# The first pair's filter step of a whitening and spectral filter kernel: six PSUM banks in turn, the soft threshold on ScalarE, the third pair whitened beside it

## The chip, the cores and the metric

The kernel runs on one core of one Trainium2 chip. The metric is device time in microseconds (us), the median of repeated runs. TensorE multiplies matrices into PSUM (8 banks), VectorE and ScalarE move PSUM to SBUF and do elementwise work, GpSimd does elementwise work in SBUF only, and SyncE issues the transfers. Everything is in 32-bit floats.

## The reference

The input x is (16, 56, 56, 64). First it is whitened over its 64 channels: the covariance over all tokens, a Cholesky factor, its inverse applied to each token, then gamma and beta. The second part is a block with a spectral filter:

```
h  = layer_norm(x, n1_g, n1_b)
xf = rfft2(h)                                  # over the two space axes
o1 = relu(block-diagonal complex layer(xf, w1, b1))
o2 = block-diagonal complex layer(o1, w2, b2)
y  = irfft2(softshrink(o2, 0.01))              # softshrink(v) = v - clamp(v, -lam, lam)
h  = y + h + x
out = gelu(layer_norm(h, n2_g, n2_b) @ mw1 + mb1) @ mw2 + mb2 + h
```

## The kernel before

**Tiling.** The 16 images go through in 8 pairs (PAIRS), one pair on 112 or 128 partitions. Before the first step there is a stage for all pairs: covariance, then elimination, which gives the whitening matrix wy. Then pairs 0 and 1 are whitened (SECOND_WHITEN is the list of banks of pair 1), and pair 0 is normalised.

**Steps.** After that the kernel runs `step(i)` for i = 0 to 7, then the last MLP. Each engine has its own `step` function, an order written out by hand; semaphores join them. Step i does the filter of pair i: `dft_h(i)` is already done, then `dft_w`, `layer_1`, `layer_2`, the soft threshold, `inv_w`, `inv_h`, and `dft_h(i + 1)`. Between these are spread the MLP of pair i-1 in seven slices, the transposes of pair i+2 (`transpose_x`, evicted by ScalarE's `ev_x`), the whitening of pair i+1 (`whiten`, `whiten_two`, evicted by VectorE's `ev_whiten`), and its first layer norm (`ln1_stats`, `mean_rstd`, `ln1_subtract`, `ln1_rstd`). Step 0 has no MLP beside it, and in it pair 1 is already whitened, so only the transposes of pair 2 and the norm of pair 1 stand beside the filter. Pair 2 is whitened in step 1.

**Layer 2 and soft threshold (L1137, L730, L736, L459).** Eight chunks, two at a time. TensorE writes two banks, VectorE adds the bias into `layer2` and clamps that into `clamped` (two buffers of each, L2_BUFS), and GpSimd subtracts the two into `p_y`. `y_ready` counts GpSimd's chunks; VectorE waits on it to reuse a buffer. `inv_w` (L1151) waits for all eight and is evicted by ScalarE (L1424). From layer 2 on, B_BANK gives every chunk bank 1 or 2 in turn: the other banks belong to the MLP and the whitening.

**Folded weights.** Once, in step 0 right after layer 1, TensorE computes two small products (L926, L929, in BANK_M, which is bank 3), and VectorE folds them into the MLP's bias and weights (L607, L608). ScalarE needs them before its first GELU in step 1.

**inv_h (L1183)** writes eight chunks, which VectorE adds to the residual (L758). In step 0 they lie in banks 1, 2, 4, 5, 6, 7, 1, 2 (`fin_bank`). `dft_h(1)` (L1089) reuses banks 4 to 7 as VectorE frees them, and needs all four passes of pair 1's norm (`norm1_step`). GpSimd's scaling of h (L438) waits for `dft_h` (`pe_h`); its residual (L433) stands between the scalings.

**Transfers.** SyncE loads a pair when the transposes of the pair before are done (`pe_a`).

## Time and profile before

| what | value |
|---|---|
| median of 3 runs | 781.53 us (779.47 to 782.99) |
| the profiled execution | 779.6 us |
| its span in the trace | 777.8 us |
| TensorE busy | 710.2 us, 91% |
| VectorE busy | 566.6 us, 73% |
| ScalarE busy | 388.7 us, 50% |
| GpSimd busy | 276.3 us, 36% |
| mean granted TensorE clock | 0.966 of 2.4 GHz |

The trace comes from one execution. A busy share is a mean over the whole span; the change touches the stretch from about 148 us to about 260 us, steps 0 and 1. A time below is counted from the span's start. PE is TensorE, DVE VectorE, ACT ScalarE and POOL GpSimd. L12 is line 12 of the kernel before. A granted clock of 1.00 is 2.4 GHz, of 0.50 is 1.2 GHz; a value between them is a stretch with both.

### The profile page before, as it was taken

How to read it: one execution, taken by the hardware profiler on the slowest of the kernel's cores; microseconds unless marked ns; L12 is line 12 of the kernel's file. 1: busy time of each engine (PE TensorE's matmuls, PEld its weight loads, DVE VectorE, ACT ScalarE, POOL GpSimd, SP SyncE). 2: the span in 40 equal slices, each digit the busy share in tenths (PEclk: the TensorE clock that was granted, in tenths of full speed). 3: DMA queues.
4: the chain of work that ended last, by engine and by line, in shares of the span. 5: the costliest groups of instructions: out<-in, count | busy, mean ns of one | idle time of the engine just before them, and what ended most of it. 6: DMA issues, size and time to landing. Idle time of an engine off the chain costs nothing.

```text
span 777.8 us, 29382 instructions
## 1 busy us (share of the span) xinstructions
PE 710.2 (91%) x12889; PEld 449.3 (58%) x12889; DVE 566.6 (73%) x1845; ACT 388.7 (50%) x709; POOL 276.3 (36%) x158
## 2 busy tenths in 40 slices
PE   6988999777789999999999999999999889899797
PEld 5986556746655665565555655555556555545343
DVE  4565998958789677967895879587958894951651
ACT  0012004642376657565765566566656545746265
POOL 7000000672564064406541563256235524560000
PEclk9898999897999999999999999999999999989989
DMA  9964000303000300030003000400100000001011
GB/s 247 269 154 144 3 3 5 82 3 84 3 3 25 109 27 15 27 109 27 15 27 109 27 14 26 114 32 5 37 27 27 9 32 25 27 15 37 13 44 63
DMA packets 11089, 40.07 MB, mean 52 GB/s; under 512 B 1955, under 2 KB 2083, under 8 KB 9507
## 3 DMA queue, kind: packets, MB, share of 16 engines
q1 hardware_dynamic: 10962, 38.20, 17.0%
q8 instruction: 102, 1.67, 0.9%
q14 instruction: 25, 0.20, 0.1%
HBM read 25.35 MB, written 12.85 MB: 49 GB/s over the span
## 4 chain that ended last, share of the span: by engine, by line
PE 64%; DVE 21%; ACT 8%; issue 5%; DMA 0%; POOL 0%; DVEq 0%; ACTq 0%
PE psum L1207 9%; PE psum L1216 9%; DVE stats L626 7%; PE psum L1183 6%; ACT o_g L1418 5%; PE psum L1151 5%; PE psum L1105 4%; PE psum L885 4%; PE psum L1089 3%; DVE layer L730 3%; PE psum L1196 3%; PE psum L936 3%; PE psum L1137 3%; PE psum L1225 3%; DVE oslice L745 2%
## 5 line engine op out<-in xcount | busy, mean ns | idle before, releaser
L1441 ACT ACTIVATE hid<-psum,hbias 128x448 f32<-128x448 f32 x224 | 124.8, 635 | 67.3 <-PE psum L1207 67.3
L1207 PE MATMUL psum<-n2T,mw1s 64*128 64x448 f32 x448 | 105.6, 583 | 6.9 <-ACT o_g L1418 6.2
L438 POOL TENSOR_TENSOR hbuf<-hbuf,prm 128x896 f32<-128x896 f32 (+1 forms) x29 | 53.5, 1848 | 159.4 <-PE psum L1089 159.4
L459 POOL TENSOR_TENSOR p_y<-layer,clamped 128x512 f32<-128x512 f32 (+1 forms) x64 | 75.9, 1185 | 74.4 <-DVE clamped L736 74.4
L1216 PE MATMUL psum<-hid,prm 128*64 128x448 f32 x448 | 96.3, 552 | 3.7 <-DVE oslice L745 3.6
L433 POOL TENSOR_TENSOR rbuf<-ybuf,prm 128x512 f32<-128x512 f32 (+2 forms) x10 | 32.4, 3236 | 157.5 <-DVE hbuf L857 128.2
L1151 PEld LDWEIGHTS psum<-cst,p_y 58*64 58x64 f32 x2048 | 52.6, 138 | 22.5 <-issue 21.2
L1151 PE MATMUL psum<-cst,p_y 58*64 58x112 f32 x2048 | 62.7, 269 | 2.8 <-ACT o_g L1424 2.5
L1450 ACT ACTIVATE mlp_t<-psum,prm 128x448 f32<-128x448 f32 x56 | 35.5, 635 | 58.4 <-PE psum L1216 56.9
L1207 PEld LDWEIGHTS psum<-n2T,mw1s 64*128 64x128 f32 x448 | 40.5, 192 | 36.2 <-issue 25.5
L1183 PE MATMUL psum<-o_g,cst 58*128 58x448 f32 x256 | 55.6, 554 | 2.0 <-ACT o_g L1424 1.2
L1122 PE MATMUL psum<-p_y,w1s 64*128 64x435 f32 (+1 forms) x256 | 53.0, 542 | 4.4 <-ACT o_g L1418 3.9
L626 DVE BATCH_NORM_STATS2 stats<-ybuf 128x6 f32<-128x64 f32 x392 | 51.7, 205 | 0.9 <-ACT ybuf L1541 0.9
L1216 PEld LDWEIGHTS psum<-hid,prm 128*64 128x64 f32 x448 | 27.2, 136 | 42.4 <-issue 31.0
L1433 ACT COPY n2T<-psum 128x448 f32<-128x448 f32 x56 | 29.9, 533 | 42.9 <-PE psum L1196 42.6
L1137 PE MATMUL psum<-w2s,o_g 64*64 64x64 f32 x1856 | 37.6, 223 | 14.6 <-DVE layer L730 12.8
L1137 PEld LDWEIGHTS psum<-w2s,o_g 64*64 64x64 f32 x1856 | 31.7, 134 | 32.4 <-DVE layer L730 20.6
L936 PE MATMUL psum<-cst 64*64 64x128 f32 x714 | 49.9, 306 | 0.5 <-issue 0.5
L1418 ACT ACTIVATE o_g<-psum,prm 64x435 f32<-64x435 f32 (+1 forms) x80 | 49.4, 618 | 1.3
L730 DVE TENSOR_TENSOR layer<-psum,prm 128x512 f32<-128x512 f32 (+1 forms) x64 | 40.4, 632 | 11.9 <-PE psum L1137 11.8
L758 DVE TENSOR_TENSOR fbuf<-psum,fbuf 128x448 f32<-128x448 f32 x32 | 18.5, 619 | 41.8 <-PE psum L1183 41.8
L1396 ACT COPY u_r<-psum 120x464 f32<-120x464 f32 x64 | 31.6, 550 | 34.4 <-PE psum L1089 34.2
(140 smaller groups left out, 1363.0 us busy)
## 6 DMA issues: line engine op xcount, KB each, us to landing
xin<-x_dram SPq DMA_DIRECT2D x8, 1568.0 KB, 8.7
out_dram<-oslice SPq DMA_DIRECT2D x112, 112.0 KB
ybuf<-x_dram SPq DMA_DIRECT2D x2, 1568.0 KB, 16.9
fbuf<-x_dram SPq DMA_DIRECT2D x2, 1568.0 KB, 20.1
xin<-x_dram SPq DMA_DIRECT2D x4, 392.0 KB, 5.4
n<-x_dram SPq DMA_DIRECT2D x1, 1568.0 KB, 23.4
n<-x_dram SPq DMA_DIRECT2D x4, 392.0 KB, 16.4
prm<-params_dram SPq DMA_DIRECT2D x1, 646.0 KB, 3.9
```

The source lines that it names most:

```text
L438: nc.gpsimd.tensor_tensor(h4[:, j0:j1], h4[:, j0:j1], gain[:, j0:j1].unsqueeze(2).broadcast_to((RP, j1 - j0, W, 2)), ALU.mult).then_inc(h_ ...
L459: nc.gpsimd.tensor_tensor(yk, a, b, ALU.subtract).then_inc(y_ready, 1)
L626: last = nc.vector.bn_stats(stats[:, w, :], src[:, w * C:(w + 1) * C])
L730: nc.vector.tensor_tensor(layer2[:, c % L2_BUFS, 0:n].rearrange("p (k m) -> p k m", m=C), bank[B_BANK[L2 + c]][:, 0:n].rearrange("p (k m) ...
L936: nc.tensor.matmul(t[cols, 128:128 + 128], ident[rows, 0:C], ident[rows, 0:128], start=True, stop=True, skip_group_check=True)
L1137: one = nc.tensor.matmul(t[b][C * half:C * half + C, j * C:j * C + C], o_g[C * b:C * b + C, at:at + C], w2s[C * b:C * b + C, C * half:C * ...
L1151: one = nc.tensor.matmul(t[h][C * d:C * d + C, j * 112:j * 112 + 112], y_v[rows, CH // 2 * s + 4 * k + j, C * d:C * d + C], cc("invw")[row ...
L1183: one = nc.tensor.matmul(t[d][:, 0:7 * C], cc("invh")[rows, RP * m:RP * m + RP], g[rows], start=(m == 0), stop=(m == 1))
L1207: nc.tensor.matmul(t[:, 0:4 * ROWS], mw1s[C * v:C * v + C, HH * m:HH * m + HH], n2T[C * v:C * v + C, s % 2, :], start=True, stop=True).the ...
L1216: last = nc.tensor.matmul(t[C * v:C * v + C, 0:4 * ROWS], pp("mw2")[:, C * m:C * m + C], hid[:, s % 2, m, v, :], start=(m == 0), stop=(m = ...
L1418: last = nc.scalar.activation(dst, src, ACT.Relu, bias=bias)
L1441: nc.scalar.activation(hid[:, s % 2, m, v, :], bank[CH_MLP[i].bank[k]][:, 0:4 * ROWS], ACT.Gelu, bias=hbias[:, m:m + 1]).then_inc(c_act, 1)
```

## The change

All of it is in step 0 and what follows from that.

- `step(0)` becomes `first_step` on TensorE, VectorE and ScalarE, with an order of its own.
- The transposes of pair 2 and their evictions move from layer 2 and `inv_w` to between the parts of `dft_w`; they use banks 0 and 3 in turn.
- In step 0, layer 2 and `inv_w` go through six banks in turn (`FIRST_SPECTRAL`) and not two.
- The soft threshold of step 0: VectorE only adds the bias; ScalarE computes relu(-v - lam) and relu(v - lam) (`shrink_first`), the second one in place; GpSimd subtracts them. There are three pairs of buffers and they lie in `hid`, the MLP's space, which is not in use yet.
- The whitening of pair 2 moves from step 1 into step 0, between the chunks of layer 2, through banks 0 and 3 (`THIRD_WHITEN`). Steps 2 and later are as before.
- `folded_weights` moves: on TensorE from behind layer 1 to behind `inv_w`, and it waits for pair 2's whitening; on VectorE to behind layer 2's evictions and ahead of `mean_rstd(1, 0)` and pair 1's norm.
- One constant, `minus_lam`, is set by GpSimd at the start.

```diff
-    return BANK_M if i == 1 and k % 2 == 1 else BANK_X
+    return BANK_M if 0 < i < 3 and k % 2 == 1 else BANK_X
...
+THIRD_WHITEN = (BANK_X, BANK_M, BANK_X, BANK_M, BANK_X, BANK_M, BANK_X)
 WHITEN = (BANK_X, 1, 2, BANK_X, 1, 2, BANK_X)
+FIRST_SPECTRAL = ((1, 2), (6, 7), (4, 5))
...
+def whiten_bank(i, k):
+
+    return (FIRST_WHITEN, SECOND_WHITEN, THIRD_WHITEN, WHITEN)[min(i, 3)][k]
+
+
+def spectral_bank(i, k):
+
+    return FIRST_SPECTRAL[(k - L2) // 2 % 3][k % 2] if i == 0 else B_BANK[k]
...
+        def shrink_bufs(i, c):
+
+            if i == 0:
+                spare = hid[:].rearrange("p s m v n -> p (s m v n)")
+                return [spare[:, 512 * j:512 * j + 512] for j in (c % 3 * 2, c % 3 * 2 + 1)]
+            return [layer2[:, c % L2_BUFS, :], clamped[:, c % L2_BUFS, :]]
...
-                        a, b = (m[:, c % L2_BUFS, 0:n].rearrange("p (k s j) -> p k s j", s=2, j=CH) for m in (layer2, clamped))
+                        a, b = (m[:, 0:n].rearrange("p (k s j) -> p k s j", s=2, j=CH) for m in shrink_bufs(i, c))
...
-                        dve.wait_ge(r_begun, 3 * i - 2)
+                        dve.wait_ge(r_begun, 3 * i - 2 if i > 2 else 1)
...
-                            bank[(WHITEN if i > 1 else SECOND_WHITEN)[k]].rearrange("p (w c) -> p w c", c=C),
+                            bank[whiten_bank(i, k)].rearrange("p (w c) -> p w c", c=C),
...
-                        if c >= L2_BUFS or i > 0:
-
-                            dve.wait_ge(y_ready, i * 8 + c - L2_BUFS + 1)
+                        bufs = 3 if i == 0 else L2_BUFS
+                        if c >= bufs or i > 0:
+
+                            dve.wait_ge(y_ready, i * 8 + c - bufs + 1)
                         n = L2_KH[c // 2] * C
+                        value, bound = shrink_bufs(i, c)
                         nc.vector.tensor_tensor(
-                            layer2[:, c % L2_BUFS, 0:n].rearrange("p (k m) -> p k m", m=C),
-                            bank[B_BANK[L2 + c]][:, 0:n].rearrange("p (k m) -> p k m", m=C),
+                            value[:, 0:n].rearrange("p (k m) -> p k m", m=C),
+                            bank[spectral_bank(i, L2 + c)][:, 0:n].rearrange("p (k m) -> p k m", m=C),
...
+                        if i == 0:
+                            continue
                         dve.wait_ge(b_dve, i * B_DVE + b_done("dve", L2 + c))
-                        nc.vector.tensor_scalar(clamped[:, c % L2_BUFS, 0:n], layer2[:, c % L2_BUFS, 0:n], LAM, -LAM,
+                        nc.vector.tensor_scalar(bound[:, 0:n], value[:, 0:n], LAM, -LAM,
...
+                def first_step():
+
+                    ev_layer_1(0)
+                    ev_whiten(2, [0])
+                    ev_layer_2(0, [0, 1])
+                    ev_whiten(2, [1, 2])
+                    ev_layer_2(0, [2, 3])
+                    ev_whiten(2, [3, 4])
+                    ev_layer_2(0, [4, 5])
+                    ev_whiten(2, [5, 6])
+                    ev_layer_2(0, [6, 7])
+                    folded_weights()
+                    mean_rstd(1, 0)
+                    for k in range(2):
+                        ln1_subtract(1, k)
+                        ln1_rstd(1, k)
+                    ev_inv_h(0, range(8))
+                    for k in range(4):
+                        ln2_stats(0, k)
+
                 def step(i, ahead, behind):
...
-                        if i > 0:
+                        if i > 1:
...
-                    if i == 0:
-                        folded_weights()
...
-                    if i == 0:
-                        ev_inv_h(0, range(8))
-                        for k in range(4):
-                            ln2_stats(0, k)
-                        return
...
-                    pe.wait_ge(whitened, 2 * 7)
+                    pe.wait_ge(whitened, 3 * 7)
...
                             pe.wait_ge(*((whitened, 1 + 3 * k) if k < 2 else (a_act, 7 + k - 1)))
+                        elif i == 2 and k > 0:
+                            if k > 1:
...
                     for k in (2 * q + 1, 2 * q + 2):
-                        if q == 0:
+                        if i == 2:
+                            pe.wait_ge(whitened, 2 * 7 + 2 * q + 1)
...
-                                last = nc.tensor.matmul(bank[WHITEN[2 * q + 1 + v]][C * b:C * b + C, j * C:j * C + C],
+                                last = nc.tensor.matmul(bank[whiten_bank(i, 2 * q + 1 + v)][C * b:C * b + C, j * C:j * C + C],
...
+                def free_spectral(i, k):
+
+                    if i > 0:
+                        return free_b(i, k)
+                    if L2 + 6 <= k < INVW:
+                        pe.wait_ge(b_dve, b_done("dve", k - 6))
+                    if k >= INVW + 6:
+                        pe.wait_ge(b_act, b_done("act", k - 6))
+                    return bank[spectral_bank(i, k)]
+
...
-                    if k == 0 and i < PAIRS - 1:
+                    if k == 0 and 1 < i < PAIRS - 1:
                         pe.wait_ge(whitened, (i + 1) * 7 + 6)
-                    t = [free_b(i, L2 + 2 * k + b) for b in range(2)]
+                    t = [free_spectral(i, L2 + 2 * k + b) for b in range(2)]
                     for j in js:
...
-                    t = [free_b(i, INVW + 2 * k + h) for h in range(2)]
+                    t = [free_spectral(i, INVW + 2 * k + h) for h in range(2)]
...
 
+                def first_step():
+
+                    transpose_x(2, [0, 1])
+                    dft_w(0, 0)
+                    transpose_x(2, [2, 3])
+                    dft_w(0, 1)
+                    transpose_x(2, [4, 5])
+                    dft_w(0, 2)
+                    transpose_x(2, [6])
+                    layer_1(0, [0])
+                    dft_w(0, 3)
+                    layer_1(0, [2, 4, 6])
+                    whiten(2, [0])
+                    pe.wait_ge(b_act, b_done("act", L2 - 1))
+                    pe.wait_ge(b_dve, b_done("dve", L2 - 1))
+                    layer_2(0, 0, range(L2_KH[0]))
+                    layer_2(0, 1, range(L2_KH[1]))
+                    whiten_two(2, 0)
+                    layer_2(0, 2, range(L2_KH[2]))
+                    whiten_two(2, 1)
+                    layer_2(0, 3, range(L2_KH[3]))
+                    whiten_two(2, 2)
+                    for k in range(4):
+                        inv_w(0, k, range(4))
+                    folded_weights()
+                    for k in range(4):
+                        inv_h(0, k)
+                    for q in range(4):
+                        dft_h(1, q)
+
...
-                        if ahead and i > 0:
+                        if ahead and i > 1:
...
-                    if ahead and i > 0:
+                    if ahead and i > 1:
...
-                    if i == 0:
-                        folded_weights()
...
-                    if i == 0:
-                        inv_w(i, 3, range(4))
-                        for k in range(4):
-                            inv_h(i, k)
-                        for q in range(4):
-                            dft_h(i + 1, q)
-                        return
...
                     fill(3)
+
+                def shrink_first(c):
+                    n = L2_KH[c // 2] * C
+                    over, under = (m[:, 0:n] for m in shrink_bufs(0, c))
+                    act.wait_ge(b_dve, b_done("dve", L2 + c))
+                    nc.scalar.activation(under, over, ACT.Relu, bias=minus_lam[:], scale=-1.0)
+                    nc.scalar.activation(over, over, ACT.Relu, bias=minus_lam[:]).then_inc(shrunk, 1)
+
+                def first_step():
+
+                    ev_x(2, [0, 1])
+                    ev_dft_w(0, [0, 1])
+                    ev_x(2, [2, 3])
+                    ev_dft_w(0, [2, 3])
+                    ev_x(2, [4, 5])
+                    ev_dft_w(0, [4, 5])
+                    ev_x(2, [6])
+                    ev_dft_w(0, [6, 7])
+                    ev_layer_1(0)
+                    for c in range(8):
+                        shrink_first(c)
+                    ev_inv_w(0, range(8))
+                    for q in range(4):
+                        ev_dft_h(1, q)
```

## Rows read from the trace of the kernel before

**Rows 1.** Busy time by stage: us, busy us (and instructions) per engine, granted clock, DMA share, GB/s.
```profile
166.60:181.00 14.40, 8.07 (x256) 6.45 (x256) 12.25 (x19) 3.37 (x7) 9.56 (x8) 0.93 0.01 2
...
181.00:195.70 14.70, 10.99 (x260) 9.71 (x261) 10.62 (x18) 4.91 (x10) 0.00 (x0) 0.73 0.41 111
...
235.10:310.70 75.60, 72.48 (x1440) 44.39 (x1438) 59.26 (x194) 46.63 (x85) 32.74 (x19) 1.00 0.15 45
```

**Rows 2.** ScalarE in order of time: start us, us, instruction, count.
```profile
125.36 0.59 ACT L1541 COPY ybuf<-psum 128x512 f32<-128x512 f32 x1 [55.21 <-PE psum L1046]
...
160.27 6.33 ACT L1418 ACTIVATE o_g<-psum,prm 64x435 f32<-64x435 f32 x10
```

**Rows 3.** TensorE in order of time; in brackets the idle time before, and who ended it.
```profile
131.82 1.13 PE L1029 MATMUL psum<-cst,xin 112*128 112x112 f32 x8 [0.44 <-ACT xT L1390]
...
149.38 0.68 PE L1105 MATMUL psum<-cst,u_r 56*64 56x58 f32 x31 [1.12 <-ACT u_r L1396]
...
155.67 3.05 PE L1122 MATMUL psum<-p_y,w1s 64*128 64x435 f32 x8
...
164.77 0.68 PE L929 MATMUL psum<-mw1s,pilot_w 64*128 64x256 f32 x2
...
179.77 1.01 PE L1029 MATMUL psum<-cst,xin 112*128 112x112 f32 x4 [0.72 <-ACT xT L1390]
...
181.03 3.26 PE L1151 MATMUL psum<-cst,p_y 58*64 58x112 f32 x64 [0.25 <-POOL p_y L459]
...
192.78 1.76 PE L1151 MATMUL psum<-cst,p_y 58*64 58x112 f32 x64 [1.15 <-ACT o_g L1424]
...
195.70 6.53 PE L1183 MATMUL psum<-o_g,cst 58*128 58x448 f32 x32 [1.15 <-ACT o_g L1424]
```

**Rows 4.** VectorE in order of time, first step and start of the second.
```profile
168.60 0.43 DVE L736 TENSOR_SCALAR clamped<-layer 128x512 f32<-128x512 f32 x1
...
169.66 1.01 DVE L736 TENSOR_SCALAR clamped<-layer 128x512 f32<-128x512 f32 x1
...
179.82 0.24 DVE L646 TENSOR_TENSOR small<-stats 128x56 f32<-128x56 f32 x1
...
180.16 0.93 DVE L649 TENSOR_TENSOR small<-stats 128x56 f32<-128x56 f32 x1
...
183.98 2.02 DVE L687 TENSOR_TENSOR hbuf<-n,small 128x1792 f32<-128x1792 f32 x1
...
190.04 2.03 DVE L693 TENSOR_TENSOR hbuf<-hbuf,small 128x1792 f32<-128x1792 f32 x1
...
197.55 1.16 DVE L758 TENSOR_TENSOR rbuf<-psum,rbuf 128x448 f32<-128x448 f32 x2 [5.48 <-PE psum L1183]
...
210.27 2.18 DVE L646 TENSOR_TENSOR small<-stats 128x56 f32<-128x56 f32 x1
...
235.07 0.68 DVE L730 TENSOR_TENSOR layer<-psum,prm 128x512 f32<-128x512 f32 x1
```

**Rows 5.** GpSimd in order of time, first step and start of the second.
```profile
172.39 1.28 POOL L459 TENSOR_TENSOR p_y<-layer,clamped 128x512 f32<-128x512 f32 x1 [0.36 <-DVE clamped L736]
...
216.87 1.27 POOL L433 TENSOR_TENSOR fbuf<-n,prm 128x512 f32<-128x512 f32 x1
```

**Rows 6.** TensorE in order of time, step 1 around its whitening and layer 2.
```profile
226.66 1.02 PE L1207 MATMUL psum<-n2T,mw1s 64*128 64x448 f32 x4
...
228.02 1.16 PE L1064 MATMUL psum<-wy,xT 64*64 64x64 f32 x64 [0.34 <-DVE ybuf L711]
...
231.80 1.77 PE L1207 MATMUL psum<-n2T,mw1s 64*128 64x448 f32 x8
...
233.51 1.16 PE L1137 MATMUL psum<-w2s,o_g 64*64 64x64 f32 x64
```

**Rows 7.** TensorE alone in stretches of 0.5 us: busy us (instructions), granted clock, DMA share, GB/s.
```profile
178.50:179.00 0.50, 0.50 (x4) 0.84 0.00 0
...
189.00:189.50 0.50, 0.00 (x0) 0.92 0.92 258
```

More of the change, by code:

```diff
@@ L220, in build @@
         negm = sb("negm", [128, 1])
+        minus_lam = sb("minus_lam", [128, 1])
         CW = 130
@@ L423, in _ @@
                 nc.gpsimd.memset(xT[:], 0.0).then_inc(s_ones, 1)
+                nc.gpsimd.memset(minus_lam[:], -LAM).then_inc(s_ones, 1)
                 r4 = [t.rearrange("p (w j h) -> p w j h", j=CH, h=2) for t in rf]
@@ L862, in _ @@
                 first_h()
-                step(0, True, False)
+                first_step()
                 for i in range(1, PAIRS - 1):
@@ L1021, in transpose_x @@
                             pe.wait_ge(*((whitened, 1 + 3 * k) if k < 2 else (a_act, 7 + k - 1)))
+                        elif i == 2 and k > 0:
+                            if k > 1:
+                                pe.wait_ge(a_act, 2 * 7 + k - 1)
                         elif k > 0:
@@ L1042, in whiten @@
                             pe.wait_ge(b_dve, (i - 2) * B_DVE + b_done("dve", FIN + 5))
-                        t = bank[(FIRST_WHITEN, SECOND_WHITEN, WHITEN)[min(i, 2)][k]]
+                        t = bank[whiten_bank(i, k)]
                         for j in range(4):
@@ L1052, in whiten_two @@
                     for k in (2 * q + 1, 2 * q + 2):
-                        if q == 0:
+                        if i == 2:
+                            pe.wait_ge(whitened, 2 * 7 + 2 * q + 1)
+                        elif q == 0:
                             who = B_READERS[L1 + 3 + k][0]
@@ L1376, in _ @@
                     dft_h(0, q)
-                step(0, True, True, False)
+                first_step()
                 for i in range(1, PAIRS - 2):
@@ L1397, in ev_dft_h, with ev_dft_w @@
                             "p (j k s) -> p k s j", j=8, s=2)).then_inc(b_act, 1)
-                def ev_dft_w(i):
-                    for k in range(8):
+                def ev_dft_w(i, ks=range(8)):
+                    for k in ks:
                         act.wait_ge(pe_b, b_count(i, S2 + k))
@@ L1424, in ev_inv_w @@
                         nc.scalar.copy(g_v[:, :, k % 2, :, 4 * (k // 2):4 * (k // 2) + 4],
-                                       bank[B_BANK[INVW + k]][:, 0:448].rearrange("p (j w m) -> p m w j", j=4, m=2)).then_inc(b_act, 1)
+                                       bank[spectral_bank(i, INVW + k)][:, 0:448].rearrange("p (j w m) -> p m w j", j=4, m=2)).then_inc(b_act, 1)
                 def ev_n2(i, s):
@@ L1522, in step @@
                     slice_(6, lambda j: rows_next({0: 2, 1: 3}.get(j)))
-                act.wait_ge(s_ones, MEMSETS + 2)
+                act.wait_ge(s_ones, MEMSETS + 3)
                 for k in range(7):
@@ L1550, in _ @@
                     ev_dft_h(0, q)
-                step(0, True, False)
+                first_step()
                 act.wait_ge(s_mlp, 2)
```

## The prediction

> **What bounds the kernel now.** I read the spans by stage first, then the order of time on each engine between 125 and 236 us. From step 1 on, a step takes 75.6 us, in which TensorE is busy for 72.5 [rows 1]: a delay that is still there when that rhythm starts goes straight into the end. The first filter step runs with no MLP beside it, and there TensorE is busy for only 8.1 of 14.4 us (layer 2) and 11.0 of 14.7 us (inverse transform over w) [rows 1]. So what bounds it is latency, not work, and I follow who waits for whom.
>
> ScalarE's ten layer 1 evictions start at 160.27 and end at 166.6 [rows 2]; call this T. Layer 2 waits for them. Before, layer 2 then alternates with VectorE over two banks, and the last y is there at 181.0, T+14.4: the next TensorE instruction, 181.03, waits on GpSimd's last y [rows 3]. The pace in between is GpSimd's: one y chunk takes 1.28 us and another 0.36 idle for the clamp [rows 5]. The clamp takes 0.43 us alone and 1.01 while GpSimd works [rows 4]. inv_w goes from 181.03 to 195.70, with a wait of 1.15 us for ScalarE before each later part [rows 3]. Meanwhile VectorE does the second pair's norm, from 179.82 to 192.07 [rows 4]. It is then free, and idle for 5.48 us before the first inv_h eviction at 197.55; call this S [rows 4].
>
> **Third pair's transposes among dft_w.** Seven groups of transposes and seven evictions move out of layer 2 and inv_w. Two groups cost TensorE 1.13 us at 2.4 GHz, one costs 1.01 at 1.2 GHz [rows 3]. The first two groups fall into the 1.12 us idle ahead of dft_w at 149.38 [rows 3]. The other five lie in dft_w. Before, the granted clock is at the lower level there: layer_1's first eight matmuls take 3.05 us, half a 64x448 pace [rows 3], against 1.77 for eight of a similar size in step 1 [rows 6]. If filling the idle keeps the clock high, five groups cost 2.8 us and layer_1's first part gives back 1.3, dft_w some 1.5: about 0. If the clock falls all the same, five groups cost 5 us, of which the waits there can take 2: +2.8. I take 0, and keep -0.3 and +2.8. ScalarE has idle time for its seven, 0.6 us each, before the chain at 160.27.
>
> **Layer 2.** TensorE starts at T; a pair of chunks takes 1.16 us [rows 6]. VectorE evicts a chunk in 0.68 [rows 4] and has two whitening evictions of about the same size between pairs. In order: chunks 0, 1 at T+1.3 to 2.6; whitening 1, 2 ready at T+3.5, evicted by T+4.8; chunks 2, 3 by T+6.1; whitening 3, 4 by T+7.4; chunks 4, 5 by T+8.7; whitening 5, 6 by T+10; chunks 6, 7 by T+10.9. ScalarE's two sides have no row; the nearest is a copy of 128x512 in 0.59 us [rows 2], the lower bound, and GpSimd's 1.28 for such a chunk [rows 5] is the upper one for each side. I take 0.6 each, 1.2 a chunk, being nearest to the same engine's row: the last ends at T+12.3. GpSimd, without the clamp's 0.36, adds 1.3 a chunk behind it and ends at T+13.8. So y is ready at 180.4 against 181.0: only 0.6 us gained, because GpSimd sets the pace either way. At the upper bound ScalarE would pace, at 2.5 us a chunk, and y would come 6 us later still.
>
> The Trainium skill (ScalarE: Activation LUTs, Rules for kernel authors) speaks against this edit: it has such relu and min/max work on VectorE. Its cost formula there is 280 ns plus 0.833 ns an element, so 0.71 us a side; the sum by it would be some 0.5 us longer. The trace cannot show the new shape; it shows 0.59 for a plain copy [rows 2].
>
> **inv_w over six banks.** The three waits for ScalarE of 1.15 us go [rows 3]. 64 matmuls take 1.76 us at 2.4 GHz and 3.26 at 1.2 [rows 3], so the whole is 7.0 to 13.0 us. Ahead of it TensorE has nothing from about T+8.5 to T+13.8. Before, with smaller gaps, the clock fell at 178.8 and came back at 189.0, 8 us after inv_w began [rows 7]. I take half speed for six to seven of the first microseconds: 10 us. inv_w ends at 190.4, and after the last eviction inv_h can begin at 191.5, which is 4.2 us earlier than 195.70.
>
> **The new wait.** On TensorE folded_weights now stands behind inv_w. On VectorE it stands ahead of mean_rstd(1) and the four norm passes, and waits for TensorE's two products. Queued behind it: the norm, then every inv_h eviction. VectorE is done with layer 2 at T+10.9 = 177.5, and now idles until the products at about 191.5 (L929's part takes 0.68 [rows 3]). Then come two small instructions, together 0.6 by the nearest row, 0.43 for a 128x512 clamp [rows 4]; mean_rstd, 4.16 before, of which 0.68 was one instruction stretched to 0.93 beside GpSimd, so 3.5; and the norm passes from 183.98 to 192.07, 8.1 [rows 4]. 191.5 + 0.6 + 3.5 + 8.1 = 203.7. S moves from 197.55 to 203.7, **+6.1 us**. Work that was hidden by inv_w has lost its cover. dft_h of the second pair waits too: its banks are freed by these evictions.
>
> **After S.** inv_h's fourth part needs the banks of the first two evictions, S+1.2, and TensorE has then been idle for some 8 us. At 1.2 GHz it takes 3.3 rather than 1.65 us (1.65 is a fourth of the 6.53 us row [rows 3]), so dft_h starts at about S+4.5, and its first quarter ends 0.7 to 0.8 us later after S than before. GpSimd's scaling and residual follow that, and the small VectorE instructions of mean_rstd wait for them: the first takes 2.18 us at 210.27 [rows 4], and they run freely only once GpSimd's last residual, from 216.87, is over [rows 5]. +0.8.
>
> **Step 1 without whitening.** Its seven VectorE evictions and 200 TensorE instructions go. On the path that is less than their sum: n2 and layer 1 still have to come from VectorE. Between mlp_in at 226.66 and layer_2 at 233.51 lie 6.85 us [rows 6]. Without the whitening: two halves of 1.02, four GELUs and a copy on ScalarE, 1.77 for the next mlp_in: about 5.5. -1.3, and VectorE, which reaches layer 2 late by 0.4 before (235.07 against 233.51 + 1.16), is on time: -0.2 more. I take -1.5; bounds are 0 and the 4.5 us of VectorE's seven evictions.
>
> **Sum.** 0 + 6.1 + 0.8 - 1.5 = +5.4 us (the -0.6 and the -4.2 are inside the 6.1). The profiled execution took 779.6 us, span 777.8; it becomes 785.0. The median of the runs stands 1.9 us above it, so I forecast **786.9 us**.
>
> **Rivals.** (a) TensorE's clock stays at 2.4 GHz through inv_w: 7 us instead of 10, then +2.4 us, 783.9. For: the packed whitening before it; against: 5 us idle just ahead of it, and the fall at 178.8 with less. 0.15. (b) The end on the other side: the stretched small instructions after 210.27 meet GpSimd no more, because VectorE arrives later than GpSimd's residuals. They last 8 us before and some 1.2 free (five at the 0.24 of the row at 179.82 [rows 4]); 6.7 off gives -1.3, 780.2. It decides if GpSimd is done with its residual by S+13. Against: GpSimd's start hangs on dft_h, which S moves as well. 0.13. The Trainium skill (SBUF — State Buffer, Who interferes with whom) has the pair of engines share ports by an exclusive lock; the 0.43 against 1.01 us of the clamp [rows 4] agrees. (c) The clock stays low through the transposes and all of inv_w: +2.8 and +3.0, 792.7. 0.12. (d) ScalarE's two sides go at the upper bound: +6, 793. 0.04. The forecast itself, between +2.5 and +9 us (784.0 to 790.5), 0.50; something else, 0.06.
>
> **Chances and range.** 0.5% is 3.9 us, about what a measurement of this kernel can tell from no change; so slower begins at 785.4. Of the forecast's 0.50 I put 0.42 above it; with (c), (d) and some of the rest, slower has 0.60. The remaining 0.08, (a) and half of (b) give 0.31 for the same; faster has 0.09. The likeliest case's own range is 784.0 to 790.5; the range to hold 8 in 10 goes from 780.0, the value of (b), to 793.0, that of (c) and (d); past it lie their far halves and what I have not named.
>
> **What would show it.** VectorE idle for 12 to 15 us ahead of the folded weights (L607), released by TensorE; the norm passes after inv_w and not beside it; the first inv_h eviction near 204; TensorE idle for 7 to 9 us within inv_h; the last y near 180.4, with GpSimd's chunks 1.3 apart; inv_w about 10 us without a wait for ScalarE; step 1's layer 2 some 5 us later than 233.5; later steps 75.6 us as before. The forecast is wrong if y comes before 178, if VectorE's norm is not held by the folded weights, or if n2 of the first pair is ready before 226.

## The result

The changed kernel took 787.28 us (median of 4 runs, 786.94 to 791.43), the kernel before 780.52 (4 runs: the three behind the table above and one more). The ratio worked out from all these runs is 1.0103, with a 95% interval from 1.0067 to 1.0139 (the two medians alone give 1.0087): slower by 1.0%, which is above the 0.5% that a measurement can tell. The forecast was 786.9. It lies closer than it deserves: the measured difference is 6.8 us, the forecast one 5.4, and before's median is 1.0 us lower with the fourth run. The profiled execution took 786.94 us, its span is 785.0 (+7.2).

The spans by stage of the changed kernel: layer 2; then inv_w up to the first inv_h eviction; then one later step.

```profile
165.60:181.88 16.28, 7.47 (x425) 6.85 (x425) 8.36 (x15) 9.60 (x16) 9.31 (x8) 0.95 0.02 4
181.88:203.81 21.93, 14.79 (x286) 12.02 (x286) 11.44 (x22) 3.87 (x8) 0.00 (x0) 0.81 0.01 1
241.50:317.10 75.60, 71.06 (x1376) 43.34 (x1372) 57.26 (x191) 45.04 (x83) 32.70 (x19) 1.00 0.15 45
```

A stretch of 75.6 us holds one later step as before [rows 1]; counted from layer 2 to layer 2, steps 2 to 5 take 75.46 to 75.47 us, 75.44 to 75.69 before. So the loss lies ahead of them. TensorE of the changed kernel in order of time:

```profile
155.93 1.73 PE L1165 MATMUL psum<-p_y,w1s 64*128 64x435 f32 x8
...
168.66 0.50 PE L1190 MATMUL psum<-w2s,o_g 64*64 64x64 f32 x18 [1.22 <-issue]
...
172.22 0.50 PE L1190 MATMUL psum<-w2s,o_g 64*64 64x64 f32 x18 [1.46 <-issue]
...
181.88 8.94 PE L1204 MATMUL psum<-cst,p_y 58*64 58x112 f32 x256 [4.74 <-POOL p_y L480]
...
191.22 0.68 PE L967 MATMUL psum<-mw1s,pilot_w 64*128 64x256 f32 x2
191.99 4.78 PE L1236 MATMUL psum<-o_g,cst 58*128 58x448 f32 x24
205.11 3.35 PE L1236 MATMUL psum<-o_g,cst 58*128 58x448 f32 x8 [8.34 <-DVE rbuf L783]
208.39 3.54 PE L1132 MATMUL psum<-cst,hbuf 56*56 56x58 f32 x155
...
233.63 3.36 PE L1260 MATMUL psum<-n2T,mw1s 64*128 64x448 f32 x8 [3.44 <-DVE o_g L741]
...
240.36 1.16 PE L1190 MATMUL psum<-w2s,o_g 64*64 64x64 f32 x64
```

256 matmuls run through without a pause. Of the three waits of 1.15 us that the prediction counts, two stood inside inv_w, ahead of its third and fourth part, and are gone. Ahead of the second part the wait was only 0.22 us. TensorE of the kernel before:

```profile
185.45 3.27 PE L1151 MATMUL psum<-cst,p_y 58*64 58x112 f32 x64 [0.22 <-ACT o_g L1424]
189.87 1.76 PE L1151 MATMUL psum<-cst,p_y 58*64 58x112 f32 x64 [1.15 <-ACT o_g L1424]
```

The third, at 195.70 [rows 3], stands ahead of inv_h, which needs the last eviction of inv_w whatever the banks are: e2, e6 and e9 below still wait 1.17, 1.17 and 1.16 us there, and in the changed kernel the folded weights' products fill it. But inv_h, which starts at 191.99 and not at 195.70, stops after 24 matmuls for 8.34 us, for evictions. VectorE of the changed kernel over the same time says why:

```profile
191.93 0.16 DVE L628 TENSOR_TENSOR hbias<-psum,prm 128x2 f32<-128x2 f32 x1 [12.61 <-PE psum L967]
192.34 0.24 DVE L667 TENSOR_TENSOR small<-stats 128x56 f32<-128x56 f32 x1
...
195.81 2.03 DVE L708 TENSOR_TENSOR hbuf<-n,small 128x1792 f32<-128x1792 f32 x1
...
203.81 3.28 DVE L783 TENSOR_TENSOR rbuf<-psum,rbuf 128x448 f32<-128x448 f32 x6
...
216.75 2.67 DVE L667 TENSOR_TENSOR small<-stats 128x56 f32<-128x56 f32 x1
...
229.52 4.01 DVE L741 TENSOR_SCALAR o_g<-psum,prm 64x435 f32<-64x435 f32 x6
```

VectorE idles for 12.61 us, until L967 (L929 before), the folded weights' product that stands behind inv_w, is done. Only then do the second pair's norm passes begin, which ran beside inv_w before [rows 4]. In the view of the waits it is one row among many:

```profile
DVE fbuf L783 <- PE psum L1236: 43.5, 14, 8.4
...
DVE hbias L628 <- PE psum L967: 12.6, 1, 12.6
```

The first, 43.5 us, is larger but it is 14 waits of the later steps, where TensorE is the bound; 12.6 in one wait, in a stretch where TensorE is not, is the loss.

Since the kernels differ only between the first and the second step, I read every trace by five events: T, layer 2's start; y, inv_w's start; S, the first inv_h eviction; n2, the start of VectorE's layer 1 evictions behind n2 (229.52 above); L2, step 1's layer 2. T itself moved between 163.0 and 168.4 from one trace to another, e6 with 163.0 having before's code up to there; so in a single trace the stretches from T on say more than the span. e5 is not in the table: the execution that was traced took 818.0 us at a mean granted clock of 0.832, a slow one, where its other nine took 771.7 to 777.5. All in us:

| kernel | T | T to y | y to S | S to n2 | n2 to L2 | L2 to end | T to end |
|---|---|---|---|---|---|---|---|
| before | 166.66 | 14.37 | 16.52 | 24.99 | 10.97 | 544.3 | 611.1 |
| after | 165.60 | 16.28 | 21.93 | 25.71 | 10.84 | 544.6 | 619.4 |
| e1 | 164.63 | 14.28 | 12.37 | 24.79 | 12.43 | 545.0 | 608.9 |
| e2 | 167.24 | 14.39 | 11.70 | 24.77 | 12.43 | 543.2 | 606.5 |
| e3 | 164.76 | 12.52 | 20.81 | 25.65 | 12.07 | 546.6 | 617.6 |
| e4 | 163.83 | 15.87 | 21.42 | 25.72 | 10.82 | 545.0 | 618.9 |
| e6 | 162.97 | 14.35 | 14.66 | 27.94 | 12.68 | 545.5 | 615.1 |
| e7 | 167.95 | 15.43 | 11.35 | 24.46 | 10.84 | 542.3 | 604.4 |
| e8 | 168.38 | 15.98 | 10.80 | 24.79 | 10.42 | 541.4 | 603.4 |
| e9 | 164.06 | 14.38 | 10.97 | 23.85 | 10.98 | 542.1 | 602.2 |
| e10 | 164.86 | 14.08 | 11.03 | 23.96 | 9.54 | 543.1 | 601.7 |
| e11 | 165.22 | 12.62 | 11.36 | 23.41 | 11.90 | 543.0 | 602.3 |

Behind L2 all these kernels do the same work in the same order, and still that column moves by 5.2 us. Part of it is a pause of TensorE in step 1's MLP, released by nothing that the trace shows: 1.69 us in the changed kernel, 1.72, 0.43, 2.24 and 1.48 in e1 to e4, 1.81 in e6, and none at this place in before and in e7 to e11. TensorE of the changed kernel:

```profile
277.34 0.97 PE L1269 MATMUL psum<-hid,prm 128*64 128x448 f32 x4 [1.69 <-issue]
```

So a few us between two kernels in the last two columns are no effect of an edit until their medians say so too.

### The profile page after: what moved, and what is told of

Same layout as the page of the kernel before. It is cut to its first block, busy times and chain, and to the rows that moved or that the text cites. A ratio compares the mean times of both kernels' runs of the same rounds, so it can differ in the third digit from the quotient of the medians.

```text
span 785.0 us, 29380 instructions
## 1 busy us (share of the span) xinstructions
PE 706.0 (90%) x12889; PEld 447.3 (57%) x12889; DVE 559.3 (71%) x1837; ACT 397.3 (51%) x725; POOL 277.8 (35%) x159
## 4 chain that ended last, share of the span: by engine, by line
PE 63%; DVE 22%; ACT 8%; issue 6%; DMA 0%; POOL 0%; DVEq 0%; ACTq 0%
PE psum L1260 9%; PE psum L1269 8%; DVE stats L647 7%; PE psum L1236 6%; ACT o_g L1492 5%; PE psum L1204 5%; PE psum L923 4%; PE psum L1148 3%; PE psum L1132 3%; PE psum L1190 3%; PE psum L1278 3%; PE psum L974 3%; PE psum L1249 3%; DVE layer L753 2%; DVE oslice L770 2%
## 5 line engine op out<-in xcount | busy, mean ns | idle before, releaser
L480 POOL TENSOR_TENSOR p_y<-layer,clamped 128x512 f32<-128x512 f32 (+1 forms) x56 | 66.3, 1184 | 64.8 <-DVE clamped L761 64.8
L1204 PEld LDWEIGHTS psum<-cst,p_y 58*64 58x64 f32 x2048 | 52.3, 138 | 23.4 <-issue 17.8
L1236 PE MATMUL psum<-o_g,cst 58*128 58x448 f32 x256 | 57.2, 568 | 9.3 <-DVE rbuf L783 8.3
L783 DVE TENSOR_TENSOR fbuf<-psum,fbuf 128x448 f32<-128x448 f32 x32 | 18.5, 620 | 43.5 <-PE psum L1236 43.5
L1190 PEld LDWEIGHTS psum<-w2s,o_g 64*64 64x64 f32 x1856 | 32.0, 134 | 29.0 <-DVE layer L753 14.6
L1479 ACT ACTIVATE p_y<-psum,prm 128x464 f32<-128x464 f32 (+1 forms) x64 | 36.5, 611 | 19.9 <-PE psum L1148 19.9
## 6 DMA issues: line engine op xcount, KB each, us to landing
n<-x_dram SPq DMA_DIRECT2D x4, 392.0 KB, 14.1
```

The source lines that it names most:

```text
L480: nc.gpsimd.tensor_tensor(yk, a, b, ALU.subtract).then_inc(y_ready, 1)
L1190: one = nc.tensor.matmul(t[b][C * half:C * half + C, j * C:j * C + C], o_g[C * b:C * b + C, at:at + C], w2s[C * b:C * b + C, C * half:C * ...
L1204: one = nc.tensor.matmul(t[h][C * d:C * d + C, j * 112:j * 112 + 112], y_v[rows, CH // 2 * s + 4 * k + j, C * d:C * d + C], cc("invw")[row ...
L1236: one = nc.tensor.matmul(t[d][:, 0:7 * C], cc("invh")[rows, RP * m:RP * m + RP], g[rows], start=(m == 0), stop=(m == 1))
```

## The experiments

Ratios are against the kernel before, run on the same chip (its median was 777.9 to 778.6 us), with 95% intervals. All of them compute the whole result; the filler products in e8 to e11 go to a bank that holds nothing anyone still reads.

### Folded weights behind the norm (e1), and early on TensorE (e2)

e1 changes one place in VectorE's order:

```diff
     def first_step():                      # VectorE
-        folded_weights()
         mean_rstd(1, 0)
         for k in range(2):
             ln1_subtract(1, k)
             ln1_rstd(1, k)
+        folded_weights()
         ev_inv_h(0, range(8))
```

> The changed kernel with one edit: on VectorE the folded weights stand behind the second pair's norm, not ahead of it. Theory (the norm is held behind the folded weights): VectorE does the norm from about 179.3 to 191, beside inv_w, so the first inv_h eviction comes at about 193.8 instead of 203.8, and the whole is 10 us shorter, 777 us: below the kernel before (780.5). Rival (the loss is in the pauses inside layer 2 and in the low clock at step 1's first MLP product; VectorE's hold is covered): 785 us or more.

Measured: 775.58 us, ratio 0.9959 (0.9935 to 0.9983). y to S falls from 21.93 to 12.37 us. VectorE of e1, the norm now 14.6 us earlier, beside inv_w:

```profile
181.20 2.03 DVE L708 TENSOR_TENSOR hbuf<-n,small 128x1792 f32<-128x1792 f32 x1
...
189.37 0.16 DVE L628 TENSOR_TENSOR hbias<-psum,prm 128x2 f32<-128x2 f32 x1
...
191.28 1.16 DVE L783 TENSOR_TENSOR rbuf<-psum,rbuf 128x448 f32<-128x448 f32 x2 [1.42 <-PE psum L1236]
```

L628 no longer waits, and the eviction at 191.28 waits for inv_h (L1236) itself. One line's place cost 1.4% of the kernel, more than the whole loss; with it mended the change is faster than before.

e2 leaves VectorE's order and moves TensorE's side:

```diff
     whiten_two(2, 2)                       # TensorE, first_step
+    folded_weights()
 ...
     inv_w(0, ...)
-    folded_weights()
```

> The changed kernel with one edit: on TensorE the two small products stand ahead of inv_w, not behind it; VectorE's order stays. Theory: VectorE's two instructions run at about 180 and the norm behind them ends at about 191.5; same gain as the first experiment, 777 us, since it is the wait that costs and not the place in one engine's queue. inv_w then starts no later, because TensorE idles there anyway. Rival: the products delay inv_w by 1 us and the gain stays under 3 us, 784 us.

Measured: 775.1 us, 0.9975 (0.9946 to 1.0003). y to S is 11.70, and y is not delayed (T to y 14.39). TensorE of e2 shows the products in its idle time ahead of inv_w:

```profile
178.75 0.68 PE L967 MATMUL psum<-mw1s,pilot_w 64*128 64x256 f32 x2
181.63 8.69 PE L1204 MATMUL psum<-cst,p_y 58*64 58x112 f32 x256 [2.20 <-POOL p_y L480]
```

The interval just reaches 1, so e2 isn't shown to be faster than before, but it is clear of the changed kernel's. The wait is a matter of the two queues' orders against each other: either one mends it.

### The third pair's whitening back in step 1 (e3), and that with e1 (e5)

```diff
     def whiten_bank(i, k):
-        return (FIRST_WHITEN, SECOND_WHITEN, THIRD_WHITEN, WHITEN)[min(i, 3)][k]
+        return (FIRST_WHITEN, SECOND_WHITEN, WHITEN, WHITEN)[min(i, 3)][k]
     # first_step, TensorE and VectorE: no whiten(2, ..), no ev_whiten(2, ..)
     def whitened_next(*ks):
-        if i > 1:
+        if i > 0:
```

> The changed kernel with the third pair's whitening put back into step 1; all else as changed, the folded weights' wait too. Theory: without the 200 small instructions the pauses of 1.2 and 1.5 us inside layer 2 go, GpSimd sets the pace, and the last y is there 13.2 us after layer 2's start, not 16.3: 3 us gained there. In step 1 the whitening costs 0 to 1.5 us, since it fills waits. Together 784.5 to 785.5 us. Rival (moving the whitening is what the change gains by): 788 us or more.

Measured: 786.28 us, 1.0103 (1.0054 to 1.0152). The interval holds both sides' ratios, so the times decide nothing. The trace of e3 does show the parts. T to y falls to 12.52, with one pause of TensorE instead of two:

```profile
167.73 1.96 PE L1182 MATMUL psum<-w2s,o_g 64*64 64x64 f32 x114 [1.00 <-issue]
...
177.28 7.82 PE L1196 MATMUL psum<-cst,p_y 58*64 58x112 f32 x256 [7.59 <-POOL p_y L480]
...
226.56 1.16 PE L1099 MATMUL psum<-wy,xT 64*64 64x64 f32 x64 [2.15 <-DVE o_g L741]
227.85 1.65 PE L1252 MATMUL psum<-n2T,mw1s 64*128 64x448 f32 x4
229.43 1.99 PE L1099 MATMUL psum<-wy,xT 64*64 64x64 f32 x64
```

GpSimd of e3 takes the eight chunks without a gap:

```profile
168.11 9.12 POOL L480 TENSOR_TENSOR p_y<-hid 128x512 f32<-128x512 f32 x8 [4.37 <-ACT hid L1547]
```

n2 to L2 grows from 10.84 to 12.07. That the whitening itself needs this time isn't shown: TensorE idles for 2.15 us ahead of it, and then a group of four takes 1.65 us and a whitening group 1.99, against 1.02 and 1.16 before [rows 6]. So whitening in layer 2 costs 3.8 us there against this trace of the changed kernel, and 1.6 to 1.9 against those of e1, e2 and e10, whose layer 2 is the same; it saves 1.2 in step 1. From T to the end e3 is 1.8 us shorter; 2.0 are lost again behind L2, of which 0.55 is its longer pause in step 1. The rest has no cause that the trace shows.

> The first and third experiments together: folded weights behind the norm on VectorE, and the third pair's whitening in step 1 as before. Kept of the change: six banks, threshold on ScalarE, transposes among dft_w. Theory (the parts add up by stretches): layer 2 to the last y 12.5 us, y to the first inv_h eviction 12.0, to n2 24.8, to step 1's layer 2 about 11.5; together 60.8 us, against 66.9 before and 63.9 in the first experiment: 6 us under the kernel before, a ratio near 0.992. Rival (moving the whitening is worth having once the hold is gone): slower than the first experiment, ratio 0.996 or more.

Measured (e5, both edits): 772.95 us, 0.9937 (0.9912 to 0.9961). The point is on my theory's side of 0.996 and the interval just reaches it; e1's interval overlaps. Only its times are used. Where the whitening stands is worth little either way.

### The clamp back on VectorE (e4)

```diff
     # ev_layer_2
-        if i == 0:
-            continue
     # ScalarE, first_step
-        for c in range(8):
-            shrink_first(c)
```

> The changed kernel with the soft threshold as before, one clamp on VectorE, in the new buffers; nothing on ScalarE. Theory (ScalarE's two sides gain little): VectorE takes 4.1 us for a pair of chunks with its whitening, the last y is there at 16.4 us after layer 2's start against 16.3, 787 us, within 1 us of the changed kernel. Rival (two-sided threshold on ScalarE is the gain of the change): y 3 us or more later, 790 us.

Measured: 785.48 us, 1.0099 (1.0060 to 1.0137), T to y 15.87 against 16.28. Putting the threshold on ScalarE gained and cost nothing that these times can tell. The two orders have different limits, though. ScalarE and GpSimd of the changed kernel, one view for each engine:

```profile
167.54 0.72 ACT L1558 ACTIVATE hid<-hid,minus_lam 128x512 f32<-128x512 f32 x1 [1.99 <-DVE hid L753]
168.17 0.71 ACT L1559 ACTIVATE hid<-hid,minus_lam 128x512 f32<-128x512 f32 x1
```

```profile
168.95 2.53 POOL L480 TENSOR_TENSOR p_y<-hid 128x512 f32<-128x512 f32 x2 [4.91 <-ACT hid L1559]
173.53 2.52 POOL L480 TENSOR_TENSOR p_y<-hid 128x512 f32<-128x512 f32 x2 [2.05 <-ACT hid L1559]
177.09 2.52 POOL L480 TENSOR_TENSOR p_y<-hid 128x512 f32<-128x512 f32 x2 [1.04 <-ACT hid L1559]
180.05 1.77 POOL L480 TENSOR_TENSOR p_y<-hid 128x320 f32<-128x320 f32 x2 [0.44 <-ACT hid L1559]
```

Two chunks take GpSimd 2.53 us, but it idles for 2.05, 1.04 and 0.44 us between the pairs, so it doesn't set the pace; TensorE's pauses and the whitening evictions ahead of it do. In e4 VectorE, which clamps as well, works without a gap from its first eviction at 165.04 to 178.70, 3.9 us for a pair of chunks with its whitening, and is itself the limit. That both end near T+16 is chance: with ScalarE's threshold y also came at T+14.3 (e1). What ScalarE's part is worth when TensorE's pauses are short no run decides.

### The six banks alone, on the kernel before (e6)

```diff
+FIRST_SPECTRAL = ((1, 2), (6, 7), (4, 5))  # in ev_layer_2, ev_inv_w, layer_2, inv_w;
                                            # nothing else of the change
```

> The kernel before with nothing but six banks in turn for layer 2 and inv_w of the first step. Theory: the last y hardly moves (GpSimd and the clamp set the pace, 14.2 us after layer 2's start against 14.4); inv_w loses its three waits of 1.15 us, but keeps two groups of transposes; the first inv_h eviction comes 3 us earlier, ratio 0.996. Rival (the norm on VectorE, done at 192.1, now ends last): nothing under 0.998.

Measured: 778.75 us, 1.0008 (0.9980 to 1.0037). I expected 0.996; the gain is absent. Only two of the three waits that I counted can go (the one ahead of inv_h stays, 1.17 us). y to S is shorter by 1.9 us, but S to n2 longer by 3.0. The ratio is the rival's, but its reason is not what happened: VectorE is done with the norm at 188.36 and waits for inv_h.

```profile
191.98 0.62 DVE L764 TENSOR_TENSOR rbuf<-psum,rbuf 128x448 f32<-128x448 f32 x1 [3.62 <-PE psum L1199]
```

TensorE of e6:

```profile
177.32 3.26 PE L1167 MATMUL psum<-cst,p_y 58*64 58x112 f32 x64 [5.18 <-POOL p_y L465]
...
190.97 8.62 PE L1199 MATMUL psum<-o_g,cst 58*128 58x448 f32 x27 [1.15 <-issue]
```

Without the waits inside inv_w, inv_w and inv_h still run slowly: 64 matmuls take 3.26 us, against 1.76 at the faster level [rows 3]. TensorE alone in e6, in two stretches (busy us and instructions, then the granted clock, DMA share, GB/s):

```profile
177.30:188.40 11.10, 9.97 (x260) 0.72 0.55 144
...
191.00:199.50 8.50, 8.50 (x27) 0.63 0.01 2
```

It waited 5.18 us for y and then ran at 0.72 and 0.63. That gave a new theory: the clock, not the banks, is what bounds this stretch. e9 tests it.

### Filler products ahead of inv_w (e9)

```diff
     # on e6: TensorE, inv_w
+    if i == 0 and k == 0 and js[0] == 0:
+        pe.wait_ge(b_dve, b_done("dve", L2 + 3))
+        stream_low(20, 6)     # 20 x matmul(bank[6][:, 0:128], ident, ident)
     pe.wait_ge(y_ready, ...)
```

> The sixth experiment (the kernel before with six banks) and 20 products of 128x128 into a free bank ahead of inv_w, where TensorE waits 5.2 us for GpSimd; they compute nothing that is used. Theory (six banks pack TensorE's work and leave one long wait, after which inv_w and inv_h run at 1.2 GHz, and that eats what the banks gain): with the clock kept up, inv_w takes 1.77 us a part, inv_h 6.3 to 6.6 us and not 8.6 plus a pause, and the first eviction of inv_h comes 11.5 us after the last y, not 14.7: ratio 0.993. Rival (the clock has no part in it, the chain over VectorE is the bound): ratio 1.000.

Measured: 771.6 us, 0.9916 (0.9887 to 0.9945), where e6 has 1.0008. TensorE of e9 in order of time (two instructions for each filler product), and then the same two stretches as for e6:

```profile
172.83 4.64 PE L953 MATMUL psum<-cst 128*128 128x128 f32 x40
...
178.44 1.76 PE L1175 MATMUL psum<-cst,p_y 58*64 58x112 f32 x64 [0.97 <-POOL p_y L465]
...
186.66 6.28 PE L1207 MATMUL psum<-o_g,cst 58*128 58x448 f32 x32 [1.16 <-ACT o_g L1448]
```

```profile
178.40:185.50 7.10, 7.06 (x260) 1.00 0.58 154
...
186.70:192.90 6.20, 6.20 (x36) 1.00 0.14 37
```

The same matmuls run at the full clock, 1.76 us for 64. y to S falls from 14.66 to 10.97, S to n2 from 27.94 to 23.85. The clock theory is shown, by a ratio whose interval is clear of e6's and by the granted clock: twenty products whose result nobody reads gain 0.9% here. The traces alone make it look larger than it is, 12.9 us from T to the end, where the medians differ by 7.2: the traced execution of e9 was its shortest (768.1 us), and e6's has two pauses, 1.15 us in inv_h and 1.81 in step 1, where e9's has none.

### Wider whitening products (e7)

```diff
     # on e1: TensorE, layer 2 of first_step
-    whiten_two(2, q)                       # 64x64 products
+    whiten(2, [2 * q + 1, 2 * q + 2])      # 128x128 products
```

> The first experiment, with the third pair whitened in 28 products of 128x128 and not in 100 of 64x64 (fewer instructions, more columns). Theory (the pauses in layer 2 are TensorE waiting for instructions, which come too slowly in a run of small products): the pauses of 0.9 to 1.5 us go, the last y comes 13.3 us after layer 2's start, not 14.3, ratio 0.995. Rival (the pauses are from VectorE and the banks): 14.3 us or more, no gain.

Measured: 775.72 us, 0.9958 (0.9927 to 0.9990), like e1, but T to y is 15.43 and not 13.3. The theory was that many small instructions make TensorE's pauses in layer 2. TensorE of e7: the pause is there, and the fewer products take longer, 2.05 us a pair against 1.1.

```profile
170.71 0.56 PE L1192 MATMUL psum<-w2s,o_g 64*64 64x64 f32 x19 [0.92 <-issue]
171.20 2.05 PE L1089 MATMUL psum<-wy,xT 128*128 128x128 f32 x16
```

The forecast of this theory failed, but the experiment doesn't refute it. In the traces such a pause comes at every 126 to 128 matmuls, each with its weight load, or at a multiple: in the changed kernel there are 128 between the pause at 168.66 and the one at 172.22, in e1 and e2 126 between two in layer 2, in e7 636 (five times 127) from the one above to the next. That looks like a supply of instructions in portions of fixed size. Fewer instructions then move a pause and do not remove it. No run tests this.

### Filler in step 1 (e8), both fillers (e10), and filler with the whitening back (e11)

```diff
     # e8, on e1: TensorE, step 1
+    stream_low(4)
     transpose_n(i - 1, 0)
+    stream_low(10)
     # e10 = e8, and in inv_w stream_low(18, 6) as in e9
     # e11 = e5, and in inv_w stream_low(28, 6)
```

> The first experiment, with 14 products of 128x128 into an unused bank around the first transposes of n2 in step 1, where TensorE waits for VectorE; they compute nothing that is used. Theory (moving the whitening away left TensorE idle there, its clock falls, and the two MLP products take 3.36 us each and not 1.77): both run at 2.4 GHz, n2 to layer 2 takes 9.5 us and not 12.4, ratio 0.992. Rival (VectorE or ScalarE sets that stretch): 12 us, no gain.

Measured: 772.56 us, 0.9928 (0.9891 to 0.9966); n2 to L2 10.42, in e1 12.43. TensorE of e1, then of e8, around step 1's first MLP products:

```profile
220.19 3.36 PE L1260 MATMUL psum<-n2T,mw1s 64*128 64x448 f32 x8 [3.44 <-DVE o_g L741]
...
225.22 3.36 PE L1260 MATMUL psum<-n2T,mw1s 64*128 64x448 f32 x8 [0.62 <-ACT n2T L1507]
```

```profile
224.93 1.77 PE L1265 MATMUL psum<-n2T,mw1s 64*128 64x448 f32 x8
...
228.67 1.77 PE L1265 MATMUL psum<-n2T,mw1s 64*128 64x448 f32 x8 [1.38 <-ACT n2T L1516]
```

Both groups of eight are back at 1.77 us. Of the 3.2 us gained on TensorE 2.0 arrive; 1.38 is now a wait for ScalarE's copy. In the stretch the effect is shown; in the whole time it isn't, since the intervals of e8 and e1 overlap.

> The eighth experiment (folded weights behind the norm, filler in step 1) and 18 more filler products ahead of inv_w. Theory: inv_w takes 7.0 us and not 7.8 to 9.4, but the norm on VectorE then ends last, 10.5 to 11 us after the last y; ratio 0.991 to 0.992, hardly under the eighth's 0.9928. Rival (clock alone): 2.5 us more, 0.989.

Measured: 768.9 us, 0.9884 (0.9839 to 0.9928), the lowest median, 1.2% under before. The ratio is nearer to the rival's 0.989 than to my 0.991, and the interval holds both; the trace speaks for my side. inv_w takes 6.36 us, in e1 9.35 and in e8, with no filler ahead of it, 7.79, but y to S is 11.03, no less than e8's 10.80. TensorE and then VectorE of e10:

```profile
178.94 6.36 PE L1212 MATMUL psum<-cst,p_y 58*64 58x112 f32 x256 [0.60 <-POOL p_y L480]
```

```profile
189.97 4.34 DVE L783 TENSOR_TENSOR rbuf<-psum,rbuf 128x448 f32<-128x448 f32 x8
```

The eviction row carries no idle time: inv_h is ready, and VectorE, with its norm, has become what sets S. From T to the end e10 is 1.7 us shorter than e8, and the two intervals overlap: that the second filler helps is not shown.

> The fifth experiment (folded weights behind the norm, third pair's whitening in step 1) and 28 filler products ahead of inv_w. Theory: 12.5 us from layer 2's start to the last y, then 11.3 to the first inv_h eviction, set by VectorE's norm, 24.8 to n2 and 11 to 12 to step 1's layer 2; ratio 0.991. Rival (the longer stay at 2.4 GHz is given back when the clock falls later in step 1): 0.994 as in the fifth.

Measured: 769.8 us, 0.9897 (0.9845 to 0.9949). T to y 12.62, n2 to L2 11.90; it is within the interval of e10. These two and e9, which has none of the change but the banks, have overlapping intervals: that the rest of the change adds anything to banks and filler is not shown.

## Why the prediction was right, and where it was not

**Transposes among dft_w: not contradicted, but one trace can't tell the size.** The clock stayed at its upper level there: layer_1's first eight matmuls took 1.73 us, not 3.05 [rows 3], and did so in all nine traces of the table with the transposes in dft_w. But 3.05 was no fixed property of the kernel before. In e6, which has its code up to there, they took 1.73 us, and in e9, which has it too, 2.68. TensorE of e6:

```profile
153.29 1.73 PE L1128 MATMUL psum<-p_y,w1s 64*128 64x435 f32 x8
```

T came 1.06 us earlier, of which 0.74 was there already when dft_h began (142.54 against 143.28). From dft_h's start to T it takes 22.5 to 23.8 us with the transposes there, and 20.7, 22.7 and 23.4 without (e6, e9, before). The 0 of the sum lies within that.

**Layer 2: mis-sized, and with the wrong engine for the pace.** The last y was to come at T+13.8 and came at T+16.3. "GpSimd sets the pace either way" holds without whitening there: in e3 it works without a gap, and y comes at T+12.5. In the changed kernel it idles for 3.5 us between its pairs of chunks, waiting for ScalarE, which waits for VectorE's layer 2 evictions. These stand behind whitening evictions that wait 2.10, 1.07 and 1.00 us for TensorE. Two pauses of TensorE, 1.22 and 1.46 us, which the trace puts down to no one, are not in my timetable. The same code gave 14.3 (e1) and 16.0 (e8, which differs from it only later), so the size is that of one execution. ScalarE's sides were sized at 0.6 and take 0.72 and 0.71, but start 0.63 apart, so their pace was right. The Trainium skill (ScalarE: Activation LUTs, What ACT_TABLE_LOAD costs) has the formula that gave 0.71: the trace agrees with its duration. The advice in its Rules for kernel authors, to keep such work on VectorE, made no difference that e4's times could show.

**inv_w: mis-sized the other way.** 10 us forecast, 8.94 measured (7.8 to 9.4 in e1 to e4, e7 and e8). It lost two waits and not three; the forecast start of inv_h, 191.5 against 191.99, doesn't hang on the third. With y 1.5 us later, the folded weights' products came at 191.9 against the forecast's 191.5: two errors that cancel, and that is luck: with each alone, S would have come 1.5 us late or 1 us early.

**The new wait: right, term by term.** Idle until 191.93 (191.5); to mean_rstd 0.41 (0.6); mean_rstd 3.47 (3.5); norm passes 8.00 (8.1); S = 203.81 (203.7). e1 and e2 show the cause from both queues.

**After S: right.** The fourth part of inv_h took 3.35 us (3.3), dft_h began at S+4.58 (S+4.5); S to n2 grew by 0.7 (0.8). Rival (b) fell: GpSimd was late by as much as VectorE, and the small instruction at 216.75 took 2.67 us, even longer than the 2.18 of [rows 4].

**Step 1 without whitening: the step that failed.** It was to give -1.5 and gave -0.1 (n2 to L2 10.84 against 10.97). I took the work away and left TensorE's pace as it was. But the whitening also kept TensorE at work there [rows 6]: in its place it idles for 3.44 us, and the next eight products run at the lower level, 3.36 us where before had 1.77 [rows 6]; in e1 and e2 the second eight do too, and n2 to L2 is 12.43. e8 shows it: with filler in that gap the stretch is 10.42, in e10 9.54, which is 1.4 under before and near the -1.5 that I had forecast. Whitening is no sure cover either: with it the stretch is 10.97 and 10.98 in before and e9, but 11.9 to 12.7 in e3, e6 and e11, where TensorE had idled for 2.1 us ahead of it and some groups ran at the lower level. The lost 1.4 us, and 0.35 between L2 and the end, make up the difference of 5.4 to 7.2 us in the span. Behind the 0.35 stand the pause of 1.69 us in step 1 that before's trace lacks, and 1.2 us that came back in the later steps, for which I have no cause.

Rival (a), the clock at 2.4 GHz through inv_w, was false for this kernel and is true of e9 and e10, where filler makes it so. Rivals (c) and (d) did not happen: the clock was up through the transposes and for part of inv_w (8.94 us, where all of it at the lower level is 13), and ScalarE's sides were far from 1.28.

## What to carry to other kernels

When a small piece of work is put behind a long one on the engine that produces it, look where the consumer stands in its own queue: here two small products behind inv_w, the last of 0.68 us, kept another engine idle for 12.6 us, and one moved line on either side gave 11 us back. Work that is removed from a gap, or a wait that is joined into one longer wait, must be priced with the clock that follows it; where the trace shows the lower clock behind a gap on the path, filler in the gap is a cheap thing to try (0.9% from e6 to e9). A stage's gain ends at the next engine: inv_w of e10 is 3.0 us shorter than that of e1, and S came only 1.3 us sooner after y, since VectorE's norm then set it. And before a few us between two single traces are called an effect, look for pauses that come and go with the same code.

## What the runs showed of the hardware

- The six banks, which removed two waits of 1.15 us, gained nothing alone (1.0008): after a wait of 5.18 us TensorE ran at 0.72 of its clock from 177.3 to 188.4 and at 0.63 from 191.0 to 199.5; the same order with 20 filler products ran at 1.00 and gained 0.8%.
- TensorE pauses for 0.9 to 1.5 us in layer 2's runs of 64x64 products, once or twice, with nothing in the trace that it waits for; T to y varies between 14.1 and 16.3 us among the traces with the third pair's whitening there. It also pauses without that whitening (1.00 us in e3, 0.85 in e11), and in dft_h and dft_w. Up to step 1's layer 1 the pauses of every trace in the table are 126 to 128 matmuls apart, each with a weight load, or a multiple of that (254, 378, 507, 634), so most such places pass without one. Fewer, wider products (e7) did not remove the pause. Its cause stays open.
- Two Activate instructions of 0.72 and 0.71 us, one behind the other, start 0.63 us apart: the duration of one is not the pace of many.
